# Two passes of attention and a gated feed-forward in one kernel: a batch's products with v gathered behind the next batch's second scores

## The chip, the cores and the metric

The kernel runs on one core of one Trainium2 chip. The metric is device time in microseconds (us), the median of several executions. Matrix products run on TensorE (PE in the profile, PEld for its weight loads), the other work on VectorE (DVE), ScalarE (ACT) and GpSimd (POOL); SyncE (SP) issues nearly all DMAs.

## The reference, cut to what matters

x is (32, 256, 256), the context ctx (32, 256, 192), all float32; there are 16 heads of 64 columns.

```python
def attention(xq, xkv, wq, wk, wv, wo, bo):
    q, k, v = heads(xq @ wq), heads(xkv @ wk), heads(xkv @ wv)
    attn = softmax(einsum("bihd,bjhd->bhij", q, k) * 64 ** -0.5)
    return einsum("bhij,bjhd->bihd", attn, v).reshape(B, S, 1024) @ wo + bo

h = layernorm(x, ln1);  x = attention(h, h, sa_w...) + x          # self
h = layernorm(x, ln2);  x = attention(h, ctx, ca_w...) + x        # cross
h = layernorm(x, ln3);  a, g = split(h @ ff_w1 + ff_b1)
out = (a * gelu(g)) @ ff_w2 + ff_b2 + x
```

## The kernel before

**Precision and tiling.** Every float32 operand of a large product is split in two, a rounded part (`_hi`, fp32r, written by ScalarE) and the remainder (`_lo`, by VectorE as a subtraction), and a product is three matmuls: hi·hi, hi·lo, lo·hi. Probabilities times v is not split.

**Batches and steps.** The two attention passes are one run over 64 "batches": 0 to 31 self-attention (sa), 32 to 63 cross-attention (ca). Iteration t works on batch t ("cur"), on leftovers of batch t-1 ("prv") and on preparations of batch t+1 ("nxt"). An iteration has four steps; step n begins with `scores(t, 2n)` and `scores(t, 2n+1)`, each for a pair of heads (L597 ff.). Then come *units*, one PSUM bank each, in the order of `STEP_UNITS`: `qk m`, the projection of q and k for head pair m (12 matmuls of 256 columns; 11 in ca, whose context has 192 columns); `v c jt`, a quarter of v (6 matmuls of 512 columns; 5 in ca); `wo half`, half of the output projection (24 matmuls of 256 columns); `x`, transposes, for the first three batches only. Each step ends with one `attend`, the products with v of two head pairs (L611 to 619): 16 matmuls of 64 stationary columns, which go in two at a time. `attend(b, n)` stands two steps behind the scores that it needs, at the end of step n+2 (steps 2, 3 of its own iteration, 0, 1 of the next).

**From scores to attend.** For pair m: VectorE takes row maxima (L1021), ScalarE four exponentials with row sums (L851), VectorE inverts the sums (L1026), GpSimd multiplies (L1253), VectorE transposes 32x32 blocks (L1035), and SP moves them in four DMAs per step (`move_blocks`, L524) so that `pT` holds transposed probabilities. Two pairs of heads are alive in `probs` and two score buffers in PSUM, so `scores` of pair g waits for the exponentials of pair g-2 (L602), and for even pairs for the q/k remainders `qk_lo` of pairs g and g+1 (L601).

**PSUM.** There are 4 banks of scores, 3 banks `unit_ps` that the units rotate through (`BANK_OF`, `bank_free`), and one bank `o_ps` for attend, whose next use waits for the split of its last result (`attended_hi`, L861 on ScalarE, then `attended_lo`, L1041 on VectorE).

**A row's way to the next batch's projections.** Rows for batch t+2 are loaded (`load_rows`), normalised (L828, ScalarE), transposed in 32x32 blocks (L1012, VectorE), stored by SP to a DRAM scratch (`store_row_blocks`, L503) and read back transposed (`load_rows_transposed`, L510); ScalarE scales them (L841), splits them (L871) and VectorE makes the remainder (L1059). SP issues in order: in step n `move_blocks(t, n)`, in step 3 before it the store of the result (L535) and of the row blocks, and at the head of an iteration the context (L515) and the read-back. The first `qk` unit waits for the remainder.

Each engine runs its own hand-written list, in order; the listing below gives them. `attention_iteration` exists once per engine: SP L526, PE L734, ACT L922, DVE L1124, POOL L1275. Weights are staged in four buffers `w_stage`, split on ScalarE (L799) with remainders on VectorE (L981) or GpSimd (L1248).

Of the kernel before, what the change touches and what calls it, by code (L numbers as in the profile page):

```python
# [10 lines left out]
P = 128  # L11
D = 256
DK = D // P
S = 256
# [12 lines left out]
LOADING, FF_LOADING = 16, 12  # L27
# [6 lines left out]
BANKS = 3  # L34
MOVES = 16 * NB
STAGES = 4
# [7 lines left out]
FILL, START, STEADY, LAST, DRAIN = ("nxt",), ("cur", "nxt"), ("prv", "cur", "nxt"), ("prv", "cur"), ("prv",)  # L44
# [13 lines left out]
BANK_OF = {("v", 0, 0): 0, ("qk", 2): 2, ("qk", 3): 1, ("v", 0, 1): 0,  # L58
# [3 lines left out]
assert set(BANK_OF) == {u for u, _ in ORDER} and len(STEP_UNITS) == STEPS  # L62

# [29 lines left out]
def attended(t, n, parts):  # L93

    part, step = ("prv", n + 2) if n < 2 else ("cur", n - 2)
    return (batch_of(t, part), step) if part in parts else None


def attended_before(t, n, parts):

    if n:
        return attended(t, n - 1, parts)
    return (t - 1, 1) if "prv" in parts else None


def moved(t, n, parts):

    if n:
        return (t, n - 1) if "cur" in parts else None
    return (t - 1, STEPS - 1) if "prv" in parts else None  # L110
# [6 lines left out]
def batch_of(t, part):  # L117
    return t - 1 if part == "prv" else t if part == "cur" else t + 1
# [22 lines left out]
PIECES = (("qk", 0), ("v", 0), ("qk", 2), ("qk", 4), ("v", 1), ("qk", 6), ("wo", 0), ("wo", 1))  # L141
# [20 lines left out]
def block_kernel(nc, x, ctx, ln1_g, ln1_b, ln2_g, ln2_b, ln3_g, ln3_b, sa_wq, sa_wk, sa_wv, sa_wo, sa_bo,  # L162
# [4 lines left out]
    with stack:  # L167
# [17 lines left out]
        o_ps = psum("o_ps", [P, 2, S])  # L185
# [40 lines left out]
        pT = sb("pT", [P, 2, NB, 2, IT * ROWS * BLK])  # L226
# [46 lines left out]
        class Pass:  # L273


            def __init__(self, name, norm, x_in, x_to, has_ctx, weights, first):
                self.norm, self.x_in, self.x_to, self.has_ctx, self.first = norm, x_in, x_to, has_ctx, first
                self.weights = weights
                self.kv = 1 if has_ctx else 0
                self.pt_ld = [sem(f"{name}_pt_ld{i}") for i in range(2)]  # L280

        class Attention(NormSemaphores):
# [25 lines left out]
            def bank_free(self, eng, t, unit):  # L308

                user = user_before(t, unit, 2 * B)  # L310
                if user:
                    (kind, *rest), b = user
                    if kind == "qk":
                        at_least(eng, self.qk_lo, b * PAIRS + rest[0] + 1)
                    elif kind == "v":
                        at_least(eng, self.v_done, b * 4 + 2 * rest[0] + rest[1] + 1)
                    elif kind == "wo":
                        at_least(eng, self.wo_done, b * 2 + rest[0] + 1)
                    else:
                        at_least(eng, self.h_done, b + 1)  # L320
# [27 lines left out]
        def over_attention(eng, iteration, starting=STARTING, turning=TURNING):  # L348
# [3 lines left out]
            for t in range(1, starting + 1):  # L352
                iteration(t, STEADY, sa)
# [10 lines left out]
        def landed(b, n, home):  # L364

            ph = pass_of(b, home)
            return ph.pt_ld[n % 2], MOVES * (2 * (b - ph.first) + n // 2 + 1)
# [15 lines left out]
        def hi_last(t, n):  # L383
            return placed(t, n, {(-1, 1): [0], (-1, 3): [2], (0, 0): [4, 5], (0, 1): [6], (0, 2): [7]},
                          {(-1, 0): [0], (-1, 1): [1], (-1, 2): [2], (-1, 3): [3, 4], (0, 0): [5], (0, 2): [6], (1, 0): [7]})

        def lo_vector(t, n):

            return {(-1, 2): [0], (-1, 3): [2], (0, 0): [3], (0, 1): [5]}.get((t, n), []) if isinstance(t, int) else []

        def lo_pool(t, n):

            return placed(t, n, {(-1, 1): [0], (-1, 3): [1, 2, 3], (0, 0): [4, 5], (0, 2): [6], (0, 3): [7]},
                          {(-1, 0): [0], (-1, 1): [1], (-1, 2): [2], (-1, 3): [3, 4], (0, 0): [5], (0, 2): [6], (1, 0): [7]})
# [14 lines left out]
        def norms(t, parts, home):  # L409

            if parts == FILL:
                return [(at, sa, 0, 0)]
            if parts == START:
                return [(at, sa, 1, 0), (at, sa, 2, 2)]
            if parts == LAST:
                return [(ff, ff, 0, 0)]
            return [] if isinstance(t, int) and t + 2 >= TOTAL else [(at, pass_of(t + 2, home), t + 2, 0)]

        def blocks_ahead(t, parts):

            return parts == STEADY and not (isinstance(t, int) and t + 2 >= TOTAL)
# [26 lines left out]
        def _(sp):  # L448
            def load_piece(i):
                for slot in columns(PIECES[i])[0]:  # L450
                    w = sa.weights[slot].rearrange("(k p) n -> p k n", p=P)
                    _, cols = columns(PIECES[i])
                    if cols is None:
                        half = PIECES[i][1]
                        sp.dma_start(columns_of(w_stage, PIECES[i], slot).rearrange("p (k n) -> p k n", k=HALF),
                                     w[:, half * HALF:(half + 1) * HALF, :]).then_inc(piece_ld[i], 16)
                    else:
                        sp.dma_start(columns_of(w_stage, PIECES[i], slot), w[:, :, cols]).then_inc(piece_ld[i], 16)
# [5 lines left out]
            def load_cross_weight(slot, quarter):  # L464
# [4 lines left out]
                if w.shape[0] == DFF:  # L469
                    rows = PAIRS // 4  # L470
                    sp.dma_start(w_stage[:, slot, cols].rearrange("p (k n) -> p k n", k=rows),
                                 w.rearrange("(k p) n -> p k n", p=P)[:, quarter * rows:(quarter + 1) * rows, :]).then_inc(ca_ld, 16)
                    return
# [43 lines left out]
            def move_blocks(b, n, home):  # L517
                freed, ready = b * STEPS + n - 1, b * PAIRS + 2 * n + 2
# [4 lines left out]
                for i in range(NB):  # L523
                    sp.dma_start(pT[:, n % 2, i, :, :], blocks[i * BLK:(i + 1) * BLK, n % 2, :, :, :]).then_inc(landed(b, n, home)[0], 16)  # L524

            def attention_iteration(t, parts, home):  # L526
                if "nxt" in parts and (ph := pass_of(t + 1, home)).has_ctx:
                    load_context(ph, t + 1)
                if blocks_next(t, parts):
                    load_rows_transposed(at, t + 1, WHOLE)  # L530
                for n in range(STEPS):
                    if n == 3 and "prv" in parts:
                        ph = pass_of(t - 1, home)
                        sp.wait_ge(at.wo_done, 2 * t)
                        sp.dma_start(tiles(ph.x_to[t - 1 - ph.first]), x_out[:]).then_inc(at.stored, 16)  # L535
                    if n == 3 and blocks_ahead(t, parts):
                        store_row_blocks(at, t + 2, WHOLE)
                    if "cur" in parts:
                        ph = pass_of(t, home)
                        move_blocks(t, n, home)  # L540
                        if n == 1:
                            at_least(sp, at.xrb_done, t)

                            sp.dma_start(x_res[:], tiles(ph.x_in[t - ph.first])).then_inc(at.res_ld, 16)
                    if n == 0 and isinstance(t, int) and 0 < t <= LOADING:
                        load_cross_weight((t - 1) // 4, (t - 1) % 4)
                    if n == 1 and isinstance(t, int) and B + 2 <= t < B + 2 + FF_LOADING:
                        load_ff_weight((t - B - 2) // 4, (t - B - 2) % 4)
                    if parts == LAST and n == 2:
                        load_rows(1, tiles(x_ca[1]))  # L550
                    if parts == DRAIN and n == 0:
                        sp.wait_ge(at.xrb_done, TOTAL)
                        sp.dma_start(x_res[:], tiles(x_ca[0])).then_inc(ff.res_ld, 16)
# [3 lines left out]
            for i in range(1, len(PIECES)):  # L557
# [7 lines left out]
            over_attention(sp, attention_iteration, LOADING, FF_LOADING)  # L565
# [20 lines left out]
        def _(pe):  # L586
# [23 lines left out]
            def attend(b, n, home):  # L610
                pe.wait_ge(*landed(b, n, home))  # L611
                pe.wait_ge(at.v_done, 4 * b + (2 if n < STEPS // 2 else 4))
                at_least(pe, at.a_lo_done, b * STEPS + n)
                for i in range(2):
                    p = pT[:, n % 2, :, i, :].rearrange("p a (j h i c) -> p j h i a c", j=IT, h=2, i=IT)
                    for jt in range(IT):
                        for hd, part in enumerate((LEFT, RIGHT)):
                            last = nc.tensor.matmul(o_ps[part, i, :], v_f[:, jt, 2 * (2 * n + i) + hd, :], p[:, jt, hd],  # L618
                                                    start=jt == 0, stop=jt == IT - 1)
# [13 lines left out]
            def project_out(t, home, unit, it):  # L633

                b, half = batch_of(t, "prv"), unit[1]
                ph = pass_of(b, home)
                bank = unit_ps[:, bank_of(unit), :]
                if it == 0:
                    at.bank_free(pe, t, unit)
                    if isinstance(b, int) and b == ph.first:  # L640
                        piece_done(pe, ph, unit)
# [9 lines left out]
            def run_unit(t, home, unit, part):  # L651
# [4 lines left out]
                if unit[0] != "wo":  # L656
                    at.bank_free(pe, t, unit)
# [18 lines left out]
                elif unit[0] == "wo":  # L676
                    for it in range(IT):
                        project_out(t, home, unit, it)
# [32 lines left out]
            def transpose_rows(b):  # L711
                pe.wait_ge(ff.ln_done, b + 1)
                for k in range(DK):
                    for it in range(IT):
                        last = nc.tensor.transpose(unit_ps[:, 2, k * S + it * P:k * S + (it + 1) * P],
# [3 lines left out]
            def end_attention():  # L719

                last = TOTAL - 1
                pe.wait_ge(at.wo_done, 2 * last)
                transpose_rows(0)
                run_unit(TOTAL, ca, ("wo", 0), "prv")
# [7 lines left out]
                run_unit(TOTAL, ca, ("wo", 1), "prv")  # L732
# [9 lines left out]

# [601 lines left out]
```

## Time and profile before

| | |
|---|---|
| median of 3 executions | 2865.33 us (2865.15 to 2866.21) |
| the profiled execution | 2866.01 us, span 2864.2 us |
| TensorE busy | 2842.0 us (99%) |
| VectorE busy | 2256.3 us (79%) |
| ScalarE, GpSimd busy | 1912.3 us (67%), 1471.1 us (51%) |
| DMA | 413.32 MB, mean 144 GB/s |
| attention, then feed-forward | up to about 2310 us, then to the end |

The span is the time from the first to the last instruction of the profiled execution. Busy times of an engine are unions. Matmuls are pipelined, so their modelled durations overlap; the distance between two starts tells what one costs. A batch of self-attention takes 36.71 us from its first scores to the next batch's, a batch of cross-attention 34.91 us.

### The profile page before, as it was taken

To read this page: it belongs to the slowest core of one execution; us is meant where nothing else is said; L and a number is where in the kernel's file an instruction comes from. 1 tells how busy PE (TensorE), PEld (TensorE's weight loads), DVE (VectorE), ACT (ScalarE), POOL (GpSimd) and SP (SyncE) were. 2 spreads that over 40 slices of the span, in tenths; PEclk is the share of its full clock that TensorE was granted. 3 is DMA by queue.
4 is the path that set the end of the run, shared out by engine and by line. 5 is a ranking of instruction groups with operands and counts; after the bars stand their busy time and mean duration, and the time that the engine had idled before them with its cause. 6 is when DMAs were issued, how large, how long until landed. Compare 5 with 4: busy or idle time off the path is not lost.

```text
span 2864.2 us, 72446 instructions
## 1 busy us (share of the span) xinstructions
PE 2842.0 (99%) x25278; PEld 2485.3 (87%) x25278; DVE 2256.3 (79%) x3495; ACT 1912.3 (67%) x6041; POOL 1471.1 (51%) x1310
## 2 busy tenths in 40 slices
PE   8999999999999999999999999999999999999999
PEld 6888888888888888888888888888888889999999
DVE  6888888888888888888888888888888865555554
ACT  6677766677766776777777777777777754444443
POOL 5444444444444444765555555555555544554554
PEclk9999999999999999999999999999999999999999
DMA  5666666666666666667777776666766632222222
GB/s 147 158 162 157 156 157 159 158 154 145 151 151 154 150 148 149 161 166 177 177 172 169 173 171 169 168 164 165 168 168 163 151 100 88 73 73 84 81 73 63
DMA packets 355360, 413.32 MB, mean 144 GB/s; under 512 B 122048, under 2 KB 209472, under 8 KB 355264
## 3 DMA queue, kind: packets, MB, share of 16 engines
q1 hardware_dynamic: 345120, 395.29, 57.4%
q10 hardware_dynamic: 10144, 16.78, 1.6%
q8 instruction: 56, 0.92, 0.1%
q14 instruction: 40, 0.33, 0.0%
HBM read 94.52 MB, written 49.02 MB: 50 GB/s over the span
## 4 chain that ended last, share of the span: by engine, by line
PE 98%; DVE 1%; ACT 1%; POOL 0%; issue 0%; DMA 0%; DVEq 0%; POOLq 0%; ACTq 0%
PE unit_ps L593 54%; PE o_ps L618 17%; PE s_ps L606 14%; PE s_ps L593 12%; DVE neg_max L1021 0%; ACT probs L851 0%; DVE blocks L1035 0%; POOL probs L1253 0%; DMA x_ln<-in_x_dram 0%; ACT qk_hi L882 0%; DVE qk_lo L1046 0%; DVE hT L1016 0%; DVE hT_lo L1059 0%; ACT x_n L828 0%; ACT L828 0%
## 5 line engine op out<-in xcount | busy, mean ns | idle before, releaser
L1253 POOL TENSOR_TENSOR probs<-probs,row_inv 128x1024 f32<-128x1024 f32 x512 | 967.8, 1896 | 893.9 <-DVE row_inv L1026 893.9
L851 ACT ACTIVATE probs<-s_ps,neg_max 128x256 f32<-128x256 f32 x2048 | 950.4, 487 | 403.9 <-DVE neg_max L1021 403.4
L1021 DVE TENSOR_REDUCE neg_max<-s_ps 128x4 f32<-128x1024 f32 x512 | 616.8, 1205 | 62.8 <-PE s_ps L606 58.4
L1035 DVE STREAM_TRANSPOSE blocks<-probs 128x1024 f32<-128x1024 f32 x512 | 633.2, 1237 | 19.9 <-POOL probs L1253 19.9
L593 PE MATMUL unit_ps<-hT_hi,w_hi 128*128 128x256 f32 x2048 | 571.3, 282 | 3.0 <-DVE hT_lo L1059 2.6
L593 PE MATMUL unit_ps<-hT_hi,w_lo 128*128 128x256 f32 x2048 | 554.0, 277 | 0.0
L618 PE MATMUL o_ps<-pT,v_f 128*64 128x256 f32 x4096 | 498.5, 385 | 1.7 <-DVE a_lo L1041 1.7
L593 PE MATMUL unit_ps<-hT_lo,w_hi 128*128 128x256 f32 x1792 | 496.1, 277 | 0.0
L851 ACT ACTIVATION_READ_ACCUMULATOR probs<-s_ps,neg_max 128x1 f32 x2048 | 444.6, 217 | 0.0
L593 PE MATMUL unit_ps<-w_hi,a_hi 128*128 128x256 f32 x1536 | 430.8, 280 | 3.8 <-DVE a_lo L1041 2.8
L593 PE MATMUL unit_ps<-w_lo,a_hi 128*128 128x256 f32 x1536 | 425.7, 277 | 0.0
L593 PE MATMUL unit_ps<-w_hi,a_lo 128*128 128x256 f32 x1536 | 425.7, 277 | 0.0
L618 PEld LDWEIGHTS o_ps<-pT,v_f 128*64 128x64 f32 x4096 | 271.7, 136 | 174.6 <-issue 48.0
L1046 DVE TENSOR_TENSOR qk_lo<-unit_ps,qk_hi 128x512 fp32r<-128x512 f32 x512 | 350.8, 685 | 76.8 <-ACT qk_hi L882 62.5
L593 PEld LDWEIGHTS unit_ps<-hT_hi,w_hi 128*128 128x128 f32 x2048 | 384.3, 188 | 21.2 <-issue 1.5
L593 PEld LDWEIGHTS unit_ps<-hT_hi,w_lo 128*128 128x128 f32 x2048 | 384.6, 188 | 0.0
L593 PEld LDWEIGHTS unit_ps<-hT_lo,w_hi 128*128 128x128 f32 x1792 | 336.8, 188 | 5.7
L1268 POOL TENSOR_TENSOR a_lo<-probs,a_hi 128x256 fp32r<-128x256 f32 x256 | 188.3, 741 | 264.9 <-ACT a_hi L900 263.0
L895 ACT ACTIVATE probs<-s_ps,b_col 128x256 f32<-128x256 f32 x256 | 121.7, 476 | 300.2 <-PE s_ps L593 300.2
L606 PE MATMUL s_ps<-qk_hi 64*128 64x256 f32 x2048 | 315.2, 304 | 6.0 <-DVE qk_lo L1046 6.0
L882 ACT CAST qk_hi<-unit_ps 128x512 fp32r<-128x512 f32 x512 | 313.9, 613 | 6.4 <-PE unit_ps L593 4.6
L1080 DVE SCALAR_TENSOR_TENSOR probs<-s_ps,b_col,probs 128x256 f32<-128x256 f32 x256 | 123.4, 482 | 240.7 <-ACT probs L895 238.7
(73 smaller groups left out, 6017.8 us busy)
## 6 DMA issues: line engine op xcount, KB each, us to landing
pT<-blocks SPq DMA_DIRECT2D x1024, 256.0 KB, 4.5
rows_t_dram<-row_blocks SPq DMA_DIRECT2D x91, 256.0 KB, 4.4
rows_in<-rows_t_dram SPq DMA_DIRECT2D x91, 256.0 KB, 4.1
x_res<-in_x_dram SPq DMA_DIRECT2D x32, 256.0 KB, 4.1
x_sa_dram<-x_out SPq DMA_DIRECT2D x32, 256.0 KB, 4.3
x_ln<-x_sa_dram ACTq DMA_DIRECT2D x32, 256.0 KB, 4.9
ctx_in<-in_ctx_dram SPq DMA_DIRECT2D x32, 256.0 KB, 4.4
x_res<-x_sa_dram SPq DMA_DIRECT2D x32, 256.0 KB, 4.1
```

The lines of the kernel that those rows point to most:

```text
L593: last = nc.tensor.matmul(dst, a, b, start=start and n == 0, stop=stop and n == len(terms) - 1)
L606: last = nc.tensor.matmul(s_ps[:, m % 2, hd, it * S:(it + 1) * S], q[part, r, 0, rows], k[part, r, 1, :], start=n == 0, stop=n == 2)
L618: last = nc.tensor.matmul(o_ps[part, i, :], v_f[:, jt, 2 * (2 * n + i) + hd, :], p[:, jt, hd], start=jt == 0, stop=jt == IT - 1)
L851: op = nc.scalar.activation(probs[:, m % 2, r, :].rearrange("p (j b c) -> p j b c", j=IT, c=BLK), scored.rearrange("p (j c b) -> p j b c", ...
L882: nc.scalar.copy(qk_hi[:, unit[1] % RING, :, :], bank.rearrange("p (a s) -> p a s", a=2)).then_inc(at.qk_hi, 1)
L895: nc.scalar.activation(gate[:, m % 2, :], s_ps[:, m % 4 // 2, m % 2, S:2 * S], ACT.Gelu, bias=b1_col[:, FT + m:FT + m + 1]).then_inc(ff.ga ...
L1021: nc.vector.tensor_reduce(neg_max[:, m % RING, :], s_ps[:, m % 2, :, :].rearrange("p h (i j) -> p (h i) j", j=S), AX_X, ALU.max, negate=Tr ...
L1035: nc.vector.transpose(blocks[:, n % 2, :, m % 2, :].rearrange("p b (j r c) -> p r j b c", j=IT, c=BLK), probs[:, m % 2, :, :].rearrange("p ...
L1046: nc.vector.tensor_tensor(qk_lo[:, m % RING, :, :], unit_ps[:, bank_of(("qk", m)), :].rearrange("p (a s) -> p a s", a=2), f32(qk_hi[:, m % ...
L1080: nc.vector.scalar_tensor_tensor(hid[:, m % 2, :], s_ps[:, m % 4 // 2, m % 2, 0:S], b1_col[:, m:m + 1], gate[:, m % 2, :], ALU.add, ALU.mu ...
L1253: nc.gpsimd.tensor_tensor(probs[:, m % 2, :, :], probs[:, m % 2, :, :], row_inv[:, m % RING, :].unsqueeze(2).broadcast_to([P, ROWS, S]), A ...
L1268: nc.gpsimd.tensor_tensor(a_lo[:, m, :], hid[:, m % 2, :], f32(a_hi[:, m, :]), ALU.subtract).then_inc(ff.u_lo, 1)
```

## The change

1. **Products with v.** The four `attend` of batch t-1 stand together in step 1 of iteration t, right behind `scores(t, 2)` and `scores(t, 3)`, as units ("a", n). No other unit is in that step.
2. **Units in the three other gaps.** Step 0: qk 3, wo 1 of batch t-2 ("old"), qk 4, qk 5. Step 2: v 00, qk 6, (x), qk 7, v 01, v 10, v 11. Step 3: half of wo 0 of batch t-1, qk 0 and qk 1 of t+1, the other half of wo 0, qk 2 of t+1.
3. **Banks.** `o_ps` is gone; `unit_ps` has four banks, which attend shares. `pT` has four buffers, so `move_blocks` waits for the same attend of the batch before.
4. **SP.** `move_blocks(t, n-1)` is issued in step n, in step 0 that of batch t-1's last. `load_rows_transposed` stands ahead of it in step 0, `load_context` and the store of the result behind it. In step 3 `store_row_blocks` stands behind `move_blocks(t, 2)`, then the load of `x_res`.
5. **ScalarE.** The first `attended_hi` stands between the two exponentials of step 1, the other three behind them; the normalisation opens step 2; `scale_rows` stands between the casts of qk 4 and qk 5 in step 0; the rows' split stands behind v 10 (sa) or behind qk 7 (ca).
6. **VectorE.** `attended_lo` 0 to 2 stand in step 1 (0 behind the row statistics, 1 and 2 behind the second reciprocal and ahead of the block transpose), 3 in step 2; output halves in steps 0 and 3; three q/k remainders in steps 0 and 3, two in step 2; in sa the rows' remainder opens step 3.
7. **GpSimd.** `residual` moves to step 2; the norm's deviation stands between the two multiplications of step 1.
8. **Weights.** `w_stage` has three buffers; output weights are loaded later into the queries' place (`load_output_weight`), pieces are split in another order, loads of later weights begin in another iteration. The first two and the last two iterations have lists of their own (`units_of`, `SECOND`, `begin_end`).

```diff
-LOADING, FF_LOADING = 16, 12
+LOADING, FF_LOADING = 12, 12
+LOADS_FROM, FF_LOADS_FROM = 3, 3
-BANKS = 3
+BANKS = 4
-STAGES = 4
+STAGES = 3
 STEP_UNITS = (
-    ((("v", 0, 0), "cur"), (("qk", 2), "cur"), (("qk", 3), "cur"), (("v", 0, 1), "cur")),
-    ((("qk", 4), "cur"), (("qk", 5), "cur"), (("wo", 0), "prv")),
-    ((("v", 1, 0), "cur"), (("x",), "nxt"), (("qk", 6), "cur"), (("qk", 7), "cur"), (("v", 1, 1), "cur")),
-    ((("qk", 0), "nxt"), (("qk", 1), "nxt"), (("wo", 1), "prv")),
+    ((("qk", 3), "cur"), (("wo", 1), "old"), (("qk", 4), "cur"), (("qk", 5), "cur")),
+    ((("a", 0), "prv"), (("a", 1), "prv"), (("a", 2), "prv"), (("a", 3), "prv")),
+    ((("v", 0, 0), "cur"), (("qk", 6), "cur"), (("x",), "nxt"), (("qk", 7), "cur"), (("v", 0, 1), "cur"),
+     (("v", 1, 0), "cur"), (("v", 1, 1), "cur")),
+    ((("wo", 0), "prv"), (("qk", 0), "nxt"), (("qk", 1), "nxt"), (("qk", 2), "nxt")),
 )
+BANK_OF = {("qk", 3): 0, ("wo", 1): 3, ("qk", 4): 1, ("qk", 5): 2,
+           ("a", 0): 0, ("a", 1): 3, ("a", 2): 1, ("a", 3): 2,
+           ("v", 0, 0): 0, ("qk", 6): 3, ("x",): 2, ("qk", 7): 1, ("v", 0, 1): 0, ("v", 1, 0): 2, ("v", 1, 1): 3,
+           ("wo", 0): 1, ("qk", 0): 0, ("qk", 1): 3, ("qk", 2): 2}
...
-        o_ps = psum("o_ps", [P, 2, S])
-        pT = sb("pT", [P, 2, NB, 2, IT * ROWS * BLK])
+        pT = sb("pT", [P, STEPS, NB, 2, IT * ROWS * BLK])
...
             def move_blocks(b, n, home):
-                freed, ready = b * STEPS + n - 1, b * PAIRS + 2 * n + 2
+                freed, ready = b * STEPS + n + 1 - STEPS, b * PAIRS + 2 * n + 2
...
+                    if n == 0 and blocks_next(t, parts):
+                        load_rows_transposed(at, t + 1, WHOLE)
+                    if n and "cur" in parts:
+                        move_blocks(t, n - 1, home)
+                    elif n == 0 and "prv" in parts:
+                        move_blocks(t - 1, STEPS - 1, home)
+                    if n == 0 and "nxt" in parts and (ph := pass_of(t + 1, home)).has_ctx:
+                        load_context(ph, t + 1)
+                    if n == 0 and "old" in parts:
+                        store_output(t - 2, home)
...
                     if n == 3 and blocks_ahead(t, parts):
                         store_row_blocks(at, t + 2, WHOLE)
...
             def attend(b, n, home):
+                o = attended_bank(b, n)
                 pe.wait_ge(*landed(b, n, home))
                 pe.wait_ge(at.v_done, 4 * b + (2 if n < STEPS // 2 else 4))
-                at_least(pe, at.a_lo_done, b * STEPS + n)
...
+                    if n == 3 and "prv" in parts and "nxt" in parts:
+                        at.bank_free(pe, t, ("wo", 0))
+                        project_out(t - 1, 0, 0, home)
+                        run_unit(t, home, ("qk", 0), "nxt")
+                        run_unit(t, home, ("qk", 1), "nxt")
+                        project_out(t - 1, 0, 1, home)
+                        run_unit(t, home, ("qk", 2), "nxt")
```

## Rows read from the trace of the kernel before

**Rows 1.** The page: busy times, and the chain that ended last.

```profile
PE 2842.0 (99%) x25278; PEld 2485.3 (87%) x25278; DVE 2256.3 (79%) x3495; ACT 1912.3 (67%) x6041; POOL 1471.1 (51%) x1310
...
PE 98%; DVE 1%; ACT 1%; POOL 0%; issue 0%; DMA 0%; DVEq 0%; POOLq 0%; ACTq 0%
```

**Rows 2.** Windows, one ca and one sa batch: PE, PEld, DVE, ACT, POOL, clock, DMA.

```profile
1717.96:1752.87 34.91, 34.91 (x320) 29.45 (x318) 30.62 (x46) 26.32 (x86) 18.75 (x15) 1.00 0.69 165
166.75:203.46 36.71, 36.71 (x332) 31.10 (x330) 30.37 (x45) 25.88 (x85) 17.57 (x14) 1.00 0.65 158
```

**Rows 3.** Timeline of PE from wo over attend and scores to v: start, us.

```profile
1715.88 0.28 PE L593 MATMUL unit_ps<-w_hi,a_lo 128*128 128x256 f32 x1
1716.08 1.95 PE L618 MATMUL o_ps<-pT,v_f 128*64 128x256 f32 x16
1717.96 0.39 PE L606 MATMUL s_ps<-qk_hi 64*128 64x256 f32 x2
1718.18 0.28 PE L606 MATMUL s_ps<-qk_lo,qk_hi 64*128 64x256 f32 x2
1718.30 0.28 PE L606 MATMUL s_ps<-qk_hi,qk_lo 64*128 64x256 f32 x2
...
1719.37 0.28 PE L606 MATMUL s_ps<-qk_hi,qk_lo 64*128 64x256 f32 x2
1719.58 0.50 PE L593 MATMUL unit_ps<-w_hi,hT_hi 128*128 128x512 f32 x1
1719.91 0.39 PE L593 MATMUL unit_ps<-w_hi,hT_lo 128*128 128x512 f32 x1
1720.14 0.39 PE L593 MATMUL unit_ps<-w_lo,hT_hi 128*128 128x512 f32 x1
```

**Rows 4.** Timeline of SP: the four moves of one step.

```profile
1721.44 3.87 SPq L524 DMA_DIRECT2D pT<-blocks  x4
```

**Rows 5.** DMA issues, 1300 to 2200 us: size, median us from issue to landing.

```profile
rows_t_dram<-row_blocks SPq DMA_DIRECT2D x26, 256.0 KB, 4.5
...
rows_in<-rows_t_dram SPq DMA_DIRECT2D x26, 256.0 KB, 4.3
...
x_ca_dram<-x_out SPq DMA_DIRECT2D x25, 256.0 KB, 5.0
```

**Rows 6.** Timeline of ACT in a ca batch.

```profile
1723.08 0.51 ACT L851 ACTIVATE probs<-s_ps,neg_max 128x256 f32<-128x256 f32 x1
...
1724.89 0.64 ACT L882 CAST qk_hi<-unit_ps 128x512 fp32r<-128x512 f32 x1
...
1733.37 1.19 ACT L841 ACTIVATE hT<-rows_in,ln_bias,ln_gain 128x256 f32<-128x256 f32 x2
```

**Rows 7.** Timeline of DVE in the same batch.

```profile
1723.86 0.74 DVE L992 BATCH_NORM_STATS2 bn<-x_ln 128x6 f32<-128x256 f32 x2
1725.09 0.18 DVE L1026 RECIPROCAL row_inv<-row_sum 128x4 f32<-128x4 f32 x1 [0.48 <-ACT probs L851]
1725.56 0.69 DVE L1046 TENSOR_TENSOR qk_lo<-unit_ps,qk_hi 128x512 fp32r<-128x512 f32 x1 [0.30 <-ACT qk_hi L882]
...
1728.69 1.24 DVE L1035 STREAM_TRANSPOSE blocks<-probs 128x1024 f32<-128x1024 f32 x1
1729.85 1.19 DVE L1021 TENSOR_REDUCE neg_max<-s_ps 128x4 f32<-128x1024 f32 x1
...
1731.16 0.66 DVE L1041 TENSOR_TENSOR a_lo<-o_ps,a_hi 128x512 fp32r<-128x512 f32 x1
1731.74 0.68 DVE L1046 TENSOR_TENSOR qk_lo<-unit_ps,qk_hi 128x512 fp32r<-128x512 f32 x1
```

**Rows 8.** Timeline of POOL: one pair's multiplication.

```profile
1714.30 1.90 POOL L1253 TENSOR_TENSOR probs<-probs,row_inv 128x1024 f32<-128x1024 f32 x1 [3.29 <-DVE row_inv L1026]
```

**Rows 9.** Timeline of PE in the first and behind the last iteration.

```profile
33.57 0.58 PE L606 MATMUL s_ps<-qk_hi 64*128 64x256 f32 x2 [3.23 <-DVE qk_lo L1046]
...
2313.05 0.55 PE L593 MATMUL unit_ps<-w_hi,a_hi 128*128 128x256 f32 x1 [2.81 <-DVE a_lo L1041]
```

More of the change, by code:

```diff
@@ L90, in user_before, with units_of @@
     return None
[L93 to L110, printed above, removed]
+def units_of(t, n, parts):
+    units = [(u, part) for u, part in STEP_UNITS[n] if part in parts and (u != ("x",) or by_tensor(t + 1))]
+    early = [(("v", 0, 0), "cur"), (("v", 0, 1), "cur")]
+    if parts == FILL:
+        return [user for user in units if user[0] != ("qk", 2)]
+    if parts == START:
+        return [(("qk", 2), "cur")] + units if n == 0 else early if n == 1 else [user for user in units if user not in early]
+    return units
 def two_steps_before(b, n):
@@ L279, in __init__ @@
                 self.kv = 1 if has_ctx else 0
-                self.pt_ld = [sem(f"{name}_pt_ld{i}") for i in range(2)]
+                self.pt_ld = [sem(f"{name}_pt_ld{i}") for i in range(STEPS)]
         class Attention(NormSemaphores):
@@ L351, in over_attention @@
             iteration(0, START, sa)
-            for t in range(1, starting + 1):
+            iteration(1, SECOND, sa)
+            for t in range(2, starting + 1):
                 iteration(t, STEADY, sa)
@@ L536, in attention_iteration @@
                     if n == 3 and blocks_ahead(t, parts):
                         store_row_blocks(at, t + 2, WHOLE)
-                    if "cur" in parts:
+                    if n == 3 and "cur" in parts:
                         ph = pass_of(t, home)
[L540 to L549, printed above, removed]
+                        at_least(sp, at.xrb_done, t)
+                        sp.dma_start(x_res[:], tiles(ph.x_in[t - ph.first])).then_inc(at.res_ld, 16)
@@ L655, in run_unit @@
                 bank = unit_ps[:, bank_of(unit), :]
-                if unit[0] != "wo":
-                    at.bank_free(pe, t, unit)
+                at.bank_free(pe, t if (unit, part) in ORDER else t - 1, unit)
                 if unit[0] == "qk":
@@ L731, in end_attention, with begin_end @@
                 hidden(0, BEGUN - 1, 0)
-                run_unit(TOTAL, ca, ("wo", 1), "prv")
+                for it in range(IT):
+                    project_out(last, 1, it, ca)
+            def begin_end(t):
+                at.bank_free(pe, t + 1, ("wo", 1))
+                for it in range(IT):
+                    project_out(t - 1, 1, it, ca)
+                pe.wait_ge(at.v_done, 4 * t + 2)
+                attend(t, 0, ca)
+                pe.wait_ge(at.wo_done, 2 * t)
+                attend(t, 1, ca)
             def attention_iteration(t, parts, home):
@@ L1174, in attention_iteration @@
+                    if n == 1 and "cur" in parts:
+                        transpose_blocks(t, 2 * n, home)
+                    if n == 3 and "prv" in parts:
+                        project_out(t - 1, 0)
+                    for pair in pairs[{0: 2 if parts == START else 1, 1: 0, 2: 1, 3: 2}[n]:]:
                         qk_remainders(*pair)
-                    if "cur" in parts:
-                        transpose_blocks(t, 2 * n, home)
-                    if n == 2 and "nxt" in parts and parts != FILL:
+                    if n == 2 and blocks_ahead(t, parts):
+                        transpose_rows(at, t + 2)
```

306 lines of the change are left out of this document (177 added, 129 removed), and 3 rows, old and new, of the table BANK_OF.

## The prediction

> **What bounds the kernel now.** I read the page first: TensorE is busy 99% of the span, and the chain that ended last is PE to 98% [rows 1]. Then the windows of one batch of each pass: PE is busy all of 36.71 us in a self-attention (sa) batch and all of 34.91 us in a cross-attention (ca) batch, VectorE 30.4 and 30.6 us of them, ScalarE and GpSimd less [rows 2]. So no wait is there to be removed from a steady batch; a gain must come from PE's own seams, and a faster PE has only 4.3 us of VectorE slack per ca batch.
>
> The timeline of PE shows the seams [rows 3]. Matmuls of 256 columns follow each other at 0.11 to 0.12 us (1718.18 to 1718.30), of 512 columns at 0.23 (1719.91 to 1720.14). Where the shape of the stationary side changes it takes longer:
> - unit to attend: 1715.88 to 1716.08 is 0.20, so 0.09 extra. The block's last matmul, as long as a scores matmul (0.39), ends at 1716.08 + 1.95, so it starts at 1717.65, and seven distances between pairs take 1.57, 0.22 each; a loss of up to 0.05 in the first of them is within that rounding. Price a = 0.09 to 0.14, taken 0.14.
> - attend to scores: 1717.65 to 1717.96 is 0.31 (0.22 without a seam), and the second pair comes 0.22 behind the first instead of 0.12. Price b = 0.19 to 0.21.
> - scores to unit: 1719.37 to 1719.58 is 0.21 (0.12), and the second matmul comes 0.33 behind the first instead of 0.23. Price c = 0.20.
>
> Each of four steps pays a + b + c = 0.55, or 2.2 us a batch.
>
> **The change, part by part.** *Gathering attend.* Afterwards a batch has three scores-to-unit seams (c), three unit-to-scores seams (x), one scores-to-attend (y), one attend-to-scores (b). Neither x nor y is in the trace of before. Both are a change of shape, so from below they cost the smallest seam seen, 0.14, from above the largest, 0.21. I take x = 0.20, as its mirror c, and y = 0.14, as the entry into attend. Saved: c + 4a + 3b - 3x - y = 0.20 + 0.56 + 0.60 - 0.60 - 0.14 = 0.62, say 0.65 us a batch; bounds 0.54 and 0.82. Matmuls are the same in number and form. PE alone would take 36.06 us in sa and 34.26 in ca.
>
> *Whether the others keep up.* I laid the new lists of one batch against the durations of [rows 4 to 8]. On VectorE an instruction starts 0.08 before the shown end of the last one (1728.69 + 1.24 against 1729.85), so back to back a block transpose costs 1.16, maxima 1.11, q/k and attend remainders 0.6, statistics 0.66 [rows 7]. An exponential takes 1.81 on ScalarE (1723.08 to the cast at 1724.89), and its sums can be used 2.01 behind its start (the reciprocal at 1725.09) [rows 6, 7]; a multiplication on GpSimd takes 1.90 [rows 8].
>
> With PE steps of ca at 0, 8.3, 17.0 and 25.9 us: a0 to a3 need banks whose readers ended between 5 and 10, and blocks that land by 13; the first starts at 9.9. Both are free. v 01 (22.35) needs the copy of v 00, ready about 22.0. Scores 6 (25.9) need the remainder of qk 7, ready about 25.7. In sa the steps start at 0, 8.6, 17.3 and 27.4 and the same two points have 0.6 and 1 us to spare. So each holds, in ca by 0.2 to 0.4, provided that VectorE's list is not late at qk 5.
>
> *The way of the rows.* That is what I expect to be late. Before, SP stored the row blocks ahead of the step's moves, and the read-back was issued 8 us behind it. Now the store stands in step 3 behind `move_blocks(t, 2)`, which waits for the transpose of pair 5, and the read-back stands at the head of the next iteration; `scale_rows` stands on ScalarE ahead of the cast of qk 5. From the end of pair 5's transpose: issue latency 0.1; four moves 3.87 [rows 4]; the store 4.8, between its own 4.5 and the 5.0 of a store issued right behind four moves; 0.05; the read-back 4.2 to 4.3 [rows 5]; `scale_rows` 1.0 (its 1.19 less the overlap) and the cast 0.65 [rows 6]. Together 14.75 us to the qk 5 remainder.
>
> From there VectorE's list runs on. Remainder 0.6, maxima 2, transpose 1, maxima 3, reciprocal, statistics, attend remainder 0: at 5.3. It waits for exponential 3, which started at 4.2, until 6.2, for a1's cast until 6.6, makes two remainders (7.8), transpose 2 (8.95), maxima 4 (10.1). Exponential 4 is done at 12.25, reciprocal 12.4, GpSimd's multiplication 14.45, transpose 4 15.65, the remainder of qk 7 16.3; scores 6 are done 1.0 behind it at the earliest, maxima 6 and the context remainder end at 19.0, the transpose of pair 5 at 20.2. The circle closes: 14.75 + 20.2 = 34.95 us per batch. In ca that is longer than PE's 34.26 and about the 34.91 of before: **the gain in ca is taken back by this loop**, and 30 batches x 0.04 = 1 us more. PE would stand some 0.7 us a batch before scores 6 and v 01. In sa the loop lacks the context remainder and is about 34.6, under PE's 36.06: the full gain, 30 batches x 0.65 = 19.5 us.
>
> A rule of the Trainium skill speaks otherwise on this term: its page "DMA: Bandwidth & Descriptors", section "Anatomy of one DMA", gives 2.0 us and bytes/436e3, an estimate of 2.6 us for 256 KB, instead of the 4.5 and 4.3 that the rows show. By it the loop would be 31.2 us and never bind. The measured times decide here.
>
> *The rest.* The load of `x_res`, `residual` and the normalisation move to places with idle time on SP, GpSimd and ScalarE: 0 while GpSimd's list ends before reciprocal 4 (by 1.7 us); if that cover went, a multiplication would be late by `residual`'s length and transpose 4 with it. The moves wait for an attend a batch back: never. `move_blocks(t-1, 3)` now queues behind the wait for the store's landing, and `a3` behind it has some 2 us left. *Start and end:* the first iteration waits on PE now, the longest time 3.23 us [rows 9], bound by splits of weights and exponentials. It loses two attends as cover (3.8 us) and two splits of 1.1 us as load; the two attends and a wo half go to the end, where PE stood 2.81 us for an attend remainder [rows 9] and has more to do now. Between -4 and +5, taken +1.
>
> **Sum** against the profiled execution (2866.0): -19.5 + 1 + 1 = -17.5, so 2848.5; the median of the runs is 0.7 lower: 2848 us. FF is untouched.
>
> **Rivals.**
> 1. *The loop does not bind in ca.* For it: a store and a read-back at 4.1 each and a list 0.2 shorter take 0.7 off. Against it: the medians of [rows 5], and that two more contacts are within 0.4 us. Then ca gains 0.65 x 30 as well: about 2828. The skill's rule above makes this case. Chance 0.22.
> 2. *The loop is longer, and the kernel gets slower.* Its place is the read-back behind the store behind four moves. At 35.56 us a ca batch the sa gain is spent: that is 0.6 more than computed, and from there it decides. With each of the two DMAs 0.5 us slower the loop is 35.95: +31 in ca, and sa loses some 0.4 of its 0.65: 2888 less some, about 2890. Against it: their medians include four-move traffic already. Chance 0.10.
> 3. *The seams do not shrink.* If leaving a unit for scores costs what attend on the way cost (x = 0.40, in that PE waits to empty and then loads weights uncovered), nothing is saved, and with the loop the time is 2866 to 2868. Every seam seen costs half of that at most. Chance 0.05.
>
> **How the numbers follow.** My forecast (sa gains, ca bound by the loop between 34.7 and 35.3) has 0.63 and gives 2838 to 2860 with start and end. The range takes in rival 1 and stops short of rival 2: 2823 to 2861. Faster by over 0.2% (below 2859.6; about what a measurement of this kernel can tell from no change): 0.60 of the forecast, rival 1 and a little else, 0.83. Same: 0.07. Slower: 0.10.
>
> **What would show it.** Right: an sa batch of 36.0 to 36.1 us with no PE idle; in ca 34.7 to 35.2, with PE waiting before scores 6 for the qk remainder or before v 01, ScalarE waiting for `rows_in` ahead of `scale_rows`, and `rows_t` landing about 9 us behind pair 5's transpose. A ca batch of 34.26 says rival 1, one over 35.5 rival 2, an sa batch over 36.5 rival 3. Other ways to be wrong: ScalarE's casts late in step 2, or a first iteration that loses far more than 5 us.

## The result, and the profile after

The changed kernel takes 2886.01 us (median; 2883.97 to 2889.70) against 2865.77 us in the same comparison: a ratio of 1.0073, 95% interval 1.0058 to 1.0088. It is slower by 20 us. I had forecast 2848 us and a range of 2823 to 2861; of my cases rival 2 happened, the longer loop, though at less than its price.

The starts of each batch's first scores in the two traces tell where the time went:

| stretch | before, us | after, us | difference |
|---|---|---|---|
| to the first scores of batch 2 | 93.33 | 91.50 | -1.8 |
| batches 2 to 31 (sa) | 1101.03 | 1088.27 | -12.8 |
| batches 32 to 62 (ca) | 1082.11 | 1113.19 | +31.1 |
| from batch 63 on | 587.7 | 590.8 | +3.1 |

Without the changes of pass, an sa batch takes 36.24 us instead of 36.71 and a ca batch 35.94 us on average (35.15 to 37.45, hardly two alike) instead of the constant 34.91.

The page of the changed kernel, its chain that ended last (before [rows 1]: PE 98%):

```profile
PE 56%; issue 17%; POOL 11%; DVE 8%; DMA 3%; ACT 2%; SPq 1%; POOLq 0%; DVEq 0%; ACTq 0%
PE unit_ps L612 30%; PE s_ps L612 12%; POOL probs L1322 9%; PE unit_ps L637 7%; PE s_ps L625 7%; DVE neg_max L1076 3%; DMA rows_t_dram<-row_blocks 2%; DVE blocks L1090 2%; POOL x_rb L1309 1%; SPq L529 1%; ACT probs L885 1%; DVE qk_lo L1101 
```

TensorE has lost the chain; a store to `rows_t_dram` has entered it. The windows of one sa batch and one ca batch (columns as in [rows 2]):

```profile
599.39:635.63 36.24, 36.24 (x329) 31.62 (x328) 30.45 (x44) 26.11 (x85) 17.56 (x13) 1.00 0.63 148
1825.68:1861.96 36.28, 34.95 (x317) 30.11 (x316) 31.00 (x46) 26.26 (x86) 18.54 (x14) 1.00 0.66 159
```

In sa TensorE is busy all the time, as foreseen. In ca it is idle for 1.3 us of 36.28. The timeline of TensorE in that batch shows the seams (the changes of shape) and two waits:

```profile
1833.85 0.28 PE L612 MATMUL unit_ps<-hT_hi,w_lo 128*128 128x256 f32 x1
1834.07 0.39 PE L625 MATMUL s_ps<-qk_hi 64*128 64x256 f32 x2
1834.29 0.28 PE L625 MATMUL s_ps<-qk_lo,qk_hi 64*128 64x256 f32 x2
...
1835.48 0.28 PE L625 MATMUL s_ps<-qk_hi,qk_lo 64*128 64x256 f32 x2
1835.69 7.36 PE L637 MATMUL unit_ps<-pT,v_f 128*64 128x256 f32 x64
1842.99 0.39 PE L625 MATMUL s_ps<-qk_hi 64*128 64x256 f32 x2
...
1848.26 0.28 PE L612 MATMUL unit_ps<-hT_hi,w_lo 128*128 128x256 f32 x1
1849.68 0.50 PE L612 MATMUL unit_ps<-w_hi,hT_hi 128*128 128x512 f32 x1 [1.14 <-ACT v_f L923]
...
1853.56 0.39 PE L625 MATMUL s_ps<-qk_hi 64*128 64x256 f32 x2 [0.17 <-DVE qk_lo L1101]
```

The 64 matmuls of four attends take 7.30 us from their first start to the next scores, where four single ones took 4 x 1.88 = 7.52 plus an entry each. The two waits in square brackets stand at the two places that I named, v 01 (for the copy of v 00) and scores 6 (for the remainder of qk 7). In some batches there is a third, ahead of the fourth attend:

```profile
1727.02 5.40 PE L637 MATMUL unit_ps<-pT,v_f 128*64 128x256 f32 x48
1733.59 1.95 PE L637 MATMUL unit_ps<-pT,v_f 128*64 128x256 f32 x16 [1.17 <-issue]
```

The profile names no releaser, but the last of its four moves landed at 1733.50. SP issues them behind the read-back, which waits for the store, so they are late with the rows. In 6 of the 29 batches 33 to 61 this costs 0.24 to 1.64 us, each time with the start 0.09 us behind the landing; over all of them it is 0.17 us a batch, and the two other places are 1.36. Who waits for whom, ca batches (1300 to 2200 us), sum in us, times, longest:

```profile
ACT hT L875 <- DMA rows_in<-rows_t_dram: 39.9, 25, 2.7
...
PE unit_ps L612 <- ACT v_f L923: 22.7, 25, 1.7
```

Once per batch ScalarE stands at `scale_rows` for 1.6 us until the read-back has landed. Before, the same list held no such wait. The whole loop can be read off one turn, first VectorE (its own list, then the remainder of the next batch's qk 5):

```profile
1837.01 0.69 DVE L1101 TENSOR_TENSOR qk_lo<-unit_ps,qk_hi 128x512 fp32r<-128x512 f32 x1 [2.08 <-ACT qk_hi L917]
...
1849.36 0.15 DVE L1081 RECIPROCAL row_inv<-row_sum 128x4 f32<-128x4 f32 x1
...
1851.62 1.25 DVE L1090 STREAM_TRANSPOSE blocks<-probs 128x1024 f32<-128x1024 f32 x1 [0.79 <-POOL probs L1322]
...
1852.85 0.66 DVE L1101 TENSOR_TENSOR qk_lo<-unit_ps,qk_hi 128x512 fp32r<-128x512 f32 x1
...
1854.05 1.40 DVE L1114 TENSOR_TENSOR hT_lo<-hT,hT_hi 128x512 fp32r<-128x512 f32 x1
1855.37 1.21 DVE L1076 TENSOR_REDUCE neg_max<-s_ps 128x4 f32<-128x1024 f32 x1
...
1856.84 1.23 DVE L1090 STREAM_TRANSPOSE blocks<-probs 128x1024 f32<-128x1024 f32 x1
...
1872.67 0.69 DVE L1101 TENSOR_TENSOR qk_lo<-unit_ps,qk_hi 128x512 fp32r<-128x512 f32 x1 [1.46 <-ACT qk_hi L917]
```

then SP behind the transpose that ends at 1858.07 (start, us of issue; shown from the last of the four moves on), and ScalarE:

```profile
1860.46 1.39 SPq L529 DMA_DIRECT2D pT<-blocks  x1
1861.90 0.61 SPq L508 DMA_DIRECT2D rows_t_dram<-row_blocks  x1
1862.70 0.48 SPq L570 DMA_DIRECT2D x_res<-x_sa_dram  x1
1868.20 0.37 SPq L515 DMA_DIRECT2D rows_in<-rows_t_dram  x1
1868.77 3.68 SPq L529 DMA_DIRECT2D pT<-blocks  x4
```

```profile
1871.07 1.12 ACT L875 ACTIVATE hT<-rows_in,ln_bias,ln_gain 128x256 f32<-128x256 f32 x2 [1.32 <-DMA rows_in<-rows_t_dram]
1872.08 0.56 ACT L917 CAST qk_hi<-unit_ps 128x512 fp32r<-128x512 f32 x1
```

From 1837.01 to 1858.07 is VectorE's part, 21.06 us, from there to 1872.67 the way over SP, the DMAs and ScalarE, 14.60 us: together 35.66 us; the batch that begins during this turn, at 1861.96, took 35.65. The other turns are made in the same way. From batch 33 on VectorE's part is 20.95 to 21.27 us, mostly 21.05, and the way back is 14.1 to 16.0, 14.8 on average. What makes the batches uneven is the landing of the store, 5.6 to 7.3 us behind its issue. Landings of the changed kernel, as in [rows 5]:

```profile
rows_t_dram<-row_blocks SPq DMA_DIRECT2D x25, 256.0 KB, 6.4
x_ln<-x_sa_dram ACTq DMA_DIRECT2D x25, 256.0 KB, 6.1
...
x_res<-x_sa_dram SPq DMA_DIRECT2D x25, 256.0 KB, 6.7
...
rows_in<-rows_t_dram SPq DMA_DIRECT2D x25, 256.0 KB, 2.9
```

### The profile page after: what moved, and what is told of

Its sections match the earlier page's. It is cut to its first block, busy times and chain, and to the rows that moved or that the text cites. A ratio compares the mean times of both kernels' runs of the same rounds, so it can differ in the third digit from the quotient of the medians.

```text
span 2883.8 us, 72587 instructions
## 1 busy us (share of the span) xinstructions
PE 2827.1 (98%) x25278; PEld 2522.1 (87%) x25278; DVE 2269.3 (79%) x3495; ACT 1919.2 (67%) x6041; POOL 1463.2 (51%) x1310
## 4 chain that ended last, share of the span: by engine, by line
PE 56%; issue 17%; POOL 11%; DVE 8%; DMA 3%; ACT 2%; SPq 1%; POOLq 0%; DVEq 0%; ACTq 0%
PE unit_ps L612 30%; PE s_ps L612 12%; POOL probs L1322 9%; PE unit_ps L637 7%; PE s_ps L625 7%; DVE neg_max L1076 3%; DMA rows_t_dram<-row_blocks 2%; DVE blocks L1090 2%; POOL x_rb L1309 1%; SPq L529 1%; ACT probs L885 1%; DVE qk_lo L1101 1%; DMA rows_in<-rows_t_dram 1%; DVE hT_lo L1114 1%; POOL rstd L1301 1%
## 5 line engine op out<-in xcount | busy, mean ns | idle before, releaser
L637 PE MATMUL unit_ps<-pT,v_f 128*64 128x256 f32 x4096 | 458.3, 381 | 3.5 <-issue 3.5
L637 PEld LDWEIGHTS unit_ps<-pT,v_f 128*64 128x64 f32 x4096 | 289.2, 137 | 151.4 <-issue 7.2
L917 ACT CAST qk_hi<-unit_ps 128x512 fp32r<-128x512 f32 x512 | 304.3, 595 | 78.1 <-PE unit_ps L612 77.9
```

What stands on the lines that cost most here:

```text
L637: last = nc.tensor.matmul(o[part, i * S:(i + 1) * S], v_f[:, jt, 2 * (2 * n + i) + hd, :], p[:, jt, hd], start=jt == 0, stop=jt == IT - 1)
L917: nc.scalar.copy(qk_hi[:, unit[1] % RING, :, :], bank.rearrange("p (a s) -> p a s", a=2)).then_inc(at.qk_hi, 1)
```

## The experiments

The theory: in ca a loop over the rows' store, read-back, `scale_rows`, the cast of qk 5 and VectorE's list sets the batch. The rival: VectorE's and ScalarE's lists in steps 1 and 2 are too long by themselves.

**1. Store ahead of the moves.** SP's list in step 3, as before the change:

```diff
                 for n in range(STEPS):
+                    if n == 3 and blocks_ahead(t, parts):
+                        store_row_blocks(at, t + 2, WHOLE)
                     if n and "cur" in parts:
                         move_blocks(t, n - 1, home)
...
-                    if n == 3 and blocks_ahead(t, parts):
-                        store_row_blocks(at, t + 2, WHOLE)
```

> One part of the change undone: in step 3 SP stores the row blocks ahead of the moves of pair 5, as before. Theory (the loop over the rows' store and read-back sets a cross-attention batch): the store is issued and lands some 4 us earlier, ScalarE no longer waits for rows_in ahead of scale_rows, a ca batch falls from 35.9 to 34.4 to 34.7 us and the kernel takes 2840 to 2850 us. Rival (VectorE's list in steps 1 and 2 is too long by itself, so that the copy of v 00 and the remainder of qk 7 are late whatever the rows do): the wait for rows_in goes, but a ca batch stays above 35.4 us and the kernel above 2870 us.

Measured: 2839.41 us, ratio 0.9911 (0.9894 to 0.9927). Ca batches take 34.48 us on average, nearly all 34.41, and TensorE is busy throughout one of them:

```profile
1800.00:1834.41 34.41, 34.41 (x321) 29.95 (x320) 31.09 (x46) 26.34 (x86) 18.55 (x15) 1.00 0.70 168
```

No wait for `rows_in` or for the copy of v 00 is left among its waits. VectorE's list is the same to the instruction, and does the same work in 34.41 us: the rival is out. The landings swap their lengths: 2.4 us for the store, now alone on its way, 5.3 us for the read-back behind the moves.

**2. The cast of qk 5 ahead of `scale_rows`.**

```diff
-                        if user[0] == ("qk", 5) and blocks_next(t, parts):
-                            scale_rows(t + 1, home)
                         split_unit(t, *user)
+                        if user[0] == ("qk", 5) and blocks_next(t, parts):
+                            scale_rows(t + 1, home)
```

> ScalarE casts qk 5 ahead of scale_rows; SP's list stays as changed. Theory: the landing of the rows no longer delays the remainder of qk 5 at the head of VectorE's list, only exponential 2 behind it, so the loop loses about 1.5 to 2.5 us: a ca batch takes 34.3 to 34.7 us, with the store still landing 6 us behind its issue; the kernel takes 2838 to 2850 us. Rival (VectorE's own list): above 35.4 us a batch, above 2870 us.

Measured: 2841.66 us, ratio 0.9918 (0.9901 to 0.9935); ca batches 34.51 us on average, again mostly 34.41. The store still lands 6.1 us behind its issue. So a landing as late as this is harmless by itself; it cost because the cast for a waiting VectorE stood behind it. The room is not large: where one store took 7.25 us, the batch took 35.64.

**3. The rows' remainder away from GpSimd's multiplication.** The timelines show that L1114, with both inputs in SBUF, takes 1.40 us where it took 0.65 before; it ends at 1855.45, 0.54 us behind a GpSimd multiplication that runs from 1853.01 to 1854.91:

```profile
1853.01 1.90 POOL L1322 TENSOR_TENSOR probs<-probs,row_inv 128x1024 f32<-128x1024 f32 x1 [1.51 <-DVE row_inv L1081]
```

The edit lets GpSimd idle meanwhile (the reciprocal that releases it comes later):

```diff
                     if n != 1 and "cur" in parts:
                         transpose_blocks(t, 2 * n, home)
+                    ahead = n == 2 and "nxt" in parts and in_context
+                    if ahead:
+                        qk_remainders(*pairs[1])
+                        x_remainder(t + 1)
                     if "cur" in parts:
                         invert_sums(t, 2 * n + 1)
...
-                    for pair in pairs[{0: 2 if parts == START else 1, 1: 0, 2: 1, 3: 2}[n]:]:
+                    for pair in pairs[{0: 2 if parts == START else 1, 1: 0, 2: 2 if ahead else 1, 3: 2}[n]:]:
                         qk_remainders(*pair)
                     if n == 2 and blocks_ahead(t, parts):
                         transpose_rows(at, t + 2)
-                    if n == 2 and "nxt" in parts and in_context:
-                        x_remainder(t + 1)
```

> In ca VectorE makes the remainders of qk 7 and of the rows ahead of its second reciprocal of step 2, so that GpSimd is idle while the rows' remainder is made (two SBUF inputs, 1.40 us in each of 25 batches of the changed kernel, 0.65 before). Theory: it takes 0.65 us again and the loop is shorter by about 0.35 us (the reciprocal, and with it a multiplication, come later): a ca batch of 35.5 instead of 35.85, the kernel 2873 to 2880 us. Rival (the long remainder has nothing to do with GpSimd, or lies beside the path): it stays at 1.40 us, or the batch stays at 35.85 us.

Measured: 2863.19 us, ratio 0.9996 (0.9986 to 1.0005); a ca batch 35.11 us. VectorE's groups over hT_lo in this kernel (count | busy, mean ns):

```profile
L1114 DVE TENSOR_TENSOR hT_lo<-hT,hT_hi 128x512 fp32r<-128x512 f32 x26 | 17.5, 671 | 0.0
L1118 DVE TENSOR_TENSOR hT_lo<-ctx_in,hT_hi 128x256 fp32r<-128x256 f32 x26 | 16.2, 623 | 0.0
```

and in the changed kernel:

```profile
L1114 DVE TENSOR_TENSOR hT_lo<-hT,hT_hi 128x512 fp32r<-128x512 f32 x25 | 35.0, 1401 | 0.0
...
L1118 DVE TENSOR_TENSOR hT_lo<-ctx_in,hT_hi 128x256 fp32r<-128x256 f32 x25 | 10.2, 408 | 0.0
```

The remainder is short again, and the context remainder, the other instruction with two SBUF inputs, has become the long one, since it now stands beside the multiplication. The gain per batch is 0.83 us (35.94 to 35.11), more than twice what I expected. In the turns of this trace VectorE's part is 20.52 instead of 21.05 us, and the way of the rows 14.54 instead of 14.83 on average, nearly all of it the store, which lands 0.28 us earlier. Together that is the 0.83. Why the store lands earlier here no run shows.

**4. The store behind the load of `x_res` too.**

```diff
-                    if n == 3 and blocks_ahead(t, parts):
-                        store_row_blocks(at, t + 2, WHOLE)
...
                         sp.dma_start(x_res[:], tiles(ph.x_in[t - ph.first])).then_inc(at.res_ld, 16)
+                    if n == 3 and blocks_ahead(t, parts):
+                        store_row_blocks(at, t + 2, WHOLE)
```

> The suspected delay made larger: the store of the row blocks also stands behind the load of x_res. Theory: the store is issued about 0.8 us later and lands behind one more transfer, the loop grows by 0.8 to 1.2 us: a ca batch of 36.7 to 37.1 us, a self-attention batch from 36.24 to at most 36.7, the kernel 2908 to 2935 us. Rival (rows are not what is waited for): no change beyond 5 us.

Measured: 2889.39 us, ratio 1.0090 (1.0073 to 1.0106); a ca batch 36.06 us, 0.1 more than the changed kernel. A miss by size: what the later issue cost (0.7), the landing nearly gave back, 5.7 us instead of 6.4, so that store and loads ended together as before. This did not tell the theories apart; it showed that the order among transfers issued within a microsecond matters little.

**5. Both edits that helped.** Edits 1 and 2 together.

> The edits of the first two experiments together: SP stores the rows ahead of the moves, ScalarE casts qk 5 ahead of scale_rows. Each alone brought most ca batches to 34.41 us with no wait of TensorE. Theory: nothing is left to gain in a steady batch, the pair takes 2835 to 2841 us; what is left over single edits are the few late batches at the change of passes (36.4 and 36.0 us). Rival (the two edits act on different waits and add up): below 2830 us.

Measured: 2837.72 us (2837.69 to 2838.77), ratio 0.9903 (0.9887 to 0.9920), ca batches 34.43 us. The single edits do not add up; either one opens the loop. This version beats both kernels, by 28 and by 48 us.

**6. The load of `x_res` away from the store.** It goes to step 0 of the next iteration, behind the store of the result.

```diff
                     if n == 0 and "old" in parts:
                         store_output(t - 2, home)
+                    if n == 0 and "prv" in parts:
+                        load_residual(t - 1, home)
...
-                    if n == 3 and "cur" in parts:
-                        ph = pass_of(t, home)
-                        at_least(sp, at.xrb_done, t)
-                        sp.dma_start(x_res[:], tiles(ph.x_in[t - ph.first])).then_inc(at.res_ld, 16)
...
```

> The changed kernel with the load of x_res taken from behind the store of the row blocks to step 0 of the next iteration, behind the store of the result. Theory (the store lands 6.4 us behind its issue instead of the 4.8 assumed because loads follow it at once and share the DMA engines): it lands 0.4 to 0.8 us earlier and a ca batch loses as much: 35.3 to 35.6 us instead of 35.9, the kernel 2868 to 2878 us. Rival (the four moves ahead of it alone make it late): the landing stays at 6.0 us or more, the kernel within 5 us of 2886.

Measured: 2875.83 us, ratio 1.0036 (1.0023 to 1.0048). The store landed after 6.0 us and a ca batch took 35.55 us.

**7. The load of `x_ln` too**, on top of experiment 6. ScalarE issues it behind its first exponential.

```diff
-                    if s < 2 and parts != FILL:
+                    if s < 2 and parts not in (FILL, STEADY):
                         load_rows(sems, ph, b)
...
                     if "cur" in parts:
                         exponentials(t, 2 * n)
+                    if n == 0 and parts == STEADY:
+                        for sems, ph, b, s, _ in norms(t, parts, home):
+                            load_rows(sems, ph, b)
```

> As the one before, and ScalarE issues the load of x_ln behind exponential 0 instead of at the head of the iteration. Theory: with nothing behind the store it lands 4.5 to 5.0 us behind its issue, a ca batch takes 34.4 to 35.0 us, the kernel 2840 to 2858 us. Rival (the four moves alone): the landing stays at 6.0 us or more, the kernel above 2875 us.

Measured: 2844.85 us, ratio 0.9929 (0.9912 to 0.9945), a ca batch 34.61 us. Landings:

```profile
rows_t_dram<-row_blocks SPq DMA_DIRECT2D x26, 256.0 KB, 4.9
x_ln<-x_sa_dram ACTq DMA_DIRECT2D x26, 256.0 KB, 2.7
rows_in<-rows_t_dram SPq DMA_DIRECT2D x26, 256.0 KB, 2.9
```

With the four moves ahead and nothing issued within 3 us behind it, the store takes 4.9 us, about what I had assumed (4.8). The 1.5 us more came with the two loads behind it. The rival of experiments 6 and 7, that the moves alone make it late, is out.

**8. The kernel before, with the late store alone.**

```diff
-                    if n == 3 and blocks_ahead(t, parts):
-                        store_row_blocks(at, t + 2, WHOLE)
                     if "cur" in parts:
                         ph = pass_of(t, home)
                         move_blocks(t, n, home)
+                        if n == 3 and blocks_ahead(t, parts):
+                            store_row_blocks(at, t + 2, WHOLE)
```

> The kernel before with this one part of the change: the rows are stored behind the moves of step 3 (its moves of pairs 6 and 7), 7 us later than before. Theory (a late landing costs only where its consumer stands ahead of a waiting VectorE list; here scale_rows stands at the end of step 1, behind both casts): the rows land about 1 us behind the time at which ScalarE is ready for them, ScalarE has idle time behind, and the kernel takes 2865 to 2872 us. Rival (the late store costs by itself, wherever its consumer stands): about 1 us a batch, 2900 us or more.

Measured: 2865.02 us, ratio 0.9998 (0.9988 to 1.0008). The store lands after 5.6 us, ScalarE waits for the read-back in 14 of 25 batches, up to 1.6 us, and every ca batch still takes 34.91 us. The late store is free where its consumer stands at the end of a list.

**9. An output half at the end of step 0**, on top of experiment 5.

```diff
-    ((("qk", 3), "cur"), (("wo", 1), "old"), (("qk", 4), "cur"), (("qk", 5), "cur")),
+    ((("qk", 3), "cur"), (("qk", 4), "cur"), (("qk", 5), "cur"), (("wo", 1), "old")),
```

VectorE adds the half behind the remainders (`project_out(t - 2, 1)` moves to the end of its step 0).

> On top of both edits together: in step 0 the output half of batch t-2 stands behind qk 5 instead of between qk 3 and qk 4, and VectorE adds it behind the remainders. A self-attention batch took 36.24 us where seams alone give 36.06; the matmuls of qk 4 and qk 5 in step 0 (24) and of qk 2 in step 3 (12) follow each other at 0.1175 us instead of 0.113. Theory A (a qk unit behind an output unit is slower by its place): qk 4 and qk 5 go back to 0.113, step 0 takes 0.10 us less, an sa batch 36.14 us, the kernel 6 us less, 2832 us. Theory B (whatever stands last ahead of the scores is slower): the output half at the end takes it over, 36.24 us a batch, the kernel within 2 us of 2838.

Measured: 2843.10 us, ratio 0.9922 (0.9905 to 0.9938). An sa batch takes 36.14 us, step 0 8.63 instead of 8.74: theory A for this stretch, though not for the whole, for which it had 2832. In ca the addition stands ahead of maxima 2 in VectorE's list, so the copy of v 00 and the remainder of qk 7 are late again and a batch takes 34.67 us; the whole is 5 us slower than experiment 5. The price of the place is real, and the edit is not worth it.

## Why the prediction was wrong

**The seams: right, but for a part of the size.** In the changed kernel's timeline a unit is followed by scores at 0.22 us (1833.85 to 1834.07) and the second pair 0.22 later: x = 0.20 as taken. Scores to attend is 0.21 (1835.48 to 1835.69), and the first distance between pairs is 0.05 longer than the next, so y = 0.14 holds too. (The bounds of the saving, 0.54 and 0.82, come out at 0.52 and 0.80 with x and y both at 0.21 and both at 0.14.) The saving per batch, said to be 0.65, was 0.47 in sa (36.71 to 36.24) and, where nothing waits, 0.50 in ca (34.91 to 34.41). What I left out is in the term "matmuls are the same in number and form": a qk unit behind an output unit and ahead of scores runs at 0.1175 us a matmul instead of 0.113, 36 matmuls and 0.16 us a batch. Experiment 9 moved it and got 0.10 of it back. Why it is so no run shows.

**The step that failed is the sum of the loop, 14.75 + 20.2 = 34.95 us,** and with it "the gain in ca is taken back". That the loop was the bound, where it runs, and the two places at which TensorE loses most of the time, all held; the third place, the fourth attend, for which the prediction had "some 2 us left", did not. The loop's length was 35.66 us in the turn shown and 35.9 on average.
- *The way of the rows, 14.75, was 14.60 in that turn and 14.8 on average.* That it fits is luck, since two errors cancel in it. The store took 6.4 us instead of 4.8, because I looked at what is ahead of it on SP (four moves) and not at what is issued behind it, the loads of `x_res` and, on ScalarE's queue, of `x_ln` (experiments 6 and 7). The read-back took 2.9 instead of 4.2: four moves used to stand ahead of it, and now they are issued behind it, the first 0.6 us later. With the moves ahead of it again (experiment 1) it took 5.3.
- *VectorE's list, 20.2, was 21.06, and this is the term that made the loop longer than computed.* Nearly all of the 0.86 is one instruction, the remainder of the rows at 1.40 instead of 0.65 us, blocked by a GpSimd multiplication (experiment 3). Up to the remainder of qk 7 my times hold to 0.2 us. I had costed this instruction by its duration before, and not asked what GpSimd does beside it after the move.

A loop of 35.9 us on average against a TensorE time of 34.4 is 1.5 us of standing a batch, where I had 0.7. Between 34.91 and 35.94 the 31 ca batches lose 31 us, more than the 12.8 us that sa brought.

**The rivals.** Rival 2 had 0.10: "0.6 more than computed, and from there it decides". The measured average was 0.99 more than computed. I put both DMAs 0.5 us slower as its mechanism; the sum of the two was 0.25 slower, and most of the rest came from VectorE. Its price of 2890 us had a loss of 0.4 us per sa batch in it, which my own loop for sa, 34.6 + 1.0 = 35.6 and so under 36.06, does not give, and which did not come. Without it the price is 2878 us, and the 2886 measured is above that. Rival 1 (the loop does not bind) is what experiments 1 and 2 made true, at 2839 and 2842 us where I had said 2828, since the seams brought less. The Trainium skill's formula for a DMA gives an estimate of 2.6 us for 256 KB ("DMA: Bandwidth & Descriptors", section "Anatomy of one DMA — SWDGE (gpsimd) path"). As that heading says, it is fitted to transfers that GpSimd issues, which the prediction does not say; SP and ScalarE issue all those of the loop. It is near the rows in which little is under way ahead of the transfer, 2.4 and 2.7 to 2.9 us, and far from those right behind four moves, 4.9 to 6.7 us. It was no guide to this loop.

**The chances.** The terms of the loop had an uncertainty of 0.5 us or more, and 0.6 us decided the sign. A cycle that comes out within 2% of what it is compared with should have had far more than 0.10 on its other side.

**Start and end.** Taken +1, they were -1.8 and +3.1, together +1.3.

**The sa pass** stayed free of the loop, as said: 36.24 us without a wait in nearly all batches. Batches 2 and 30 took 36.77 and 37.07; with the store ahead of the moves (experiment 1) they take 36.24 as well. So the pass brought 12.8 us and not 30 x 0.47 = 14.1.

## What to carry to other kernels

When an order is changed, close the loops: follow each product round to the next time the same list needs it, DMAs and queue positions included, and compare the sum with the batch. Where they are within a few per cent, the sign is open. A late transfer costs nothing until its consumer stands ahead of something that another engine waits for; moving that consumer by one place, or the store by one, was worth 44 to 47 us here. And the gathered products did pay: with the loop open, fewer changes of shape are worth 0.5 us of 35 per batch.

## What the runs showed of the hardware

- A VectorE instruction with two inputs in SBUF waits for a GpSimd instruction that runs, to the end: 1.40 us instead of 0.65 in 25 of 25, ending 0.54 us behind GpSimd's. Those with an input in PSUM (`qk_lo`, 0.68 us) do not, and neither do the transposes. The Trainium skill states it, in "SBUF — State Buffer", section "SBUF: two separate sides": the shared port pair is an exclusive lock, and two SBUF inputs are enough to need it against a GpSimd instruction that reads SBUF. The trace agrees, and so does experiment 3, where the long instruction is the context remainder (0.41 to 0.62 us).
- The landing of a 256 KB transfer can depend on what is issued after it as well. The store took 2.4 us alone, 4.9 behind four moves, 6.4 behind four moves and with two loads following within 1 us. It is not so for each transfer: the read-back landed after 2.9 us though four moves followed it, the first after 0.6 us. What makes the difference no run shows.
- Changes of the stationary operand's shape cost 0.14 to 0.21 us each, in all five directions seen, the two new ones (unit to scores, scores to attend) included.
